# A five-part attention stack on one core: the transfers that are not urgent move from SyncE's queue to GpSimd's, the rows of ones and selectors are filled by DMA instead of by VectorE copies, and VectorE makes the bf16 splits of the first two sets

## What is computed

```python
x = L0(x, ctx)   # 8 heads; LayerNorm of x and of ctx first; x + attention
x = L1(x, ctx)   # 16 heads; causal, keys and queries masked by the valid tokens
x = L2(x, ctx)   # 16 heads; x + attention @ Wo + bo, then x + gelu(x @ W1 + b1) @ W2 + b2
# L3: self attention (causal and padded), then cross attention, then a feed-forward
x = layernorm(mha(x, x) @ Wo1 + bo1 + x)
x = layernorm(mha(x, ctx) @ Wo2 + bo2 + x)
x = layernorm(gelu(x @ W1 + bf1) @ W2 + bf2 + x)
# all in float32; in each attention:
scores = q @ k.T / sqrt(d); probs = softmax(scores + mask); out = probs @ v
```

## Time and profile before

| what | before |
|---|---|
| median of 3 runs | 502.99 us (500.06 to 517.87) |
| the profiled execution | 502.5 us |
| its span, from the first to the last instruction | 500.7 us |
| instructions | 17180 |
| TensorE busy | 447.9 us, 89% |
| VectorE busy | 396.4 us, 79% |
| ScalarE busy | 321.8 us, 64% |
| GpSimd busy | 219.5 us, 44% |
| mean granted clock of TensorE | 0.96 |
| share of the chain that ended last: TensorE, VectorE, DMA, waiting for nothing shown, GpSimd | 72%, 13%, 5%, 4%, 3% |

### The profile page before, as it was taken

The page is one execution under the profiler, slowest core; times in us unless marked ns, Lnnn a source line. Parts: engine busy times, 40 slices in busy tenths (PEclk is TensorE's granted clock), DMA queues, the critical chain, the costliest instruction groups (busy, mean ns, idle before and its releaser), DMA issues.

```text
span 500.7 us, 17180 instructions
## 1 busy us (share of the span) xinstructions
PE 447.9 (89%) x6720; PEld 303.0 (61%) x6720; DVE 396.4 (79%) x1097; ACT 321.8 (64%) x660; POOL 219.5 (44%) x257
## 2 busy tenths in 40 slices
PE   3468869899999988899999999999999999999983
PEld 2356546566666655567777766666666666666762
DVE  7797997868887875879998777878889996777563
ACT  2235746546676654678777776657777787777851
POOL 3475566735722432345444333333443453122245
PEclk9667998999999998999999999999999999999997
DMA  8323434543433444434343232223134432220001
GB/s 189 93 63 98 108 77 92 125 103 99 108 83 79 102 87 89 107 84 96 87 106 74 62 71 65 64 64 76 31 74 93 102 75 65 66 58 14 13 22 31
DMA packets 73138, 39.99 MB, mean 80 GB/s; under 512 B 7168, under 2 KB 72928, under 8 KB 73060
## 3 DMA queue, kind: packets, MB, share of 16 engines
q1 hardware_dynamic: 72952, 38.80, 33.3%
q10 hardware_dynamic: 108, 0.10, 0.1%
HBM read 4.74 MB, written 1.05 MB: 12 GB/s over the span
## 4 chain that ended last, share of the span: by engine, by line
PE 72%; DVE 13%; DMA 5%; issue 4%; POOL 3%; ACT 2%; SPq 1%; POOLq 0%; DVEq 0%; ACTq 0%
PE attn_ps L997 16%; PE o_ps L1024 14%; PE misc_ps L1054 6%; PE misc_ps L1045 5%; PE misc_ps L959 5%; PE misc_ps L1031 4%; DMA pairs<-max_rows 4%; PE score_ps L878 4%; PE misc_ps L960 3%; DVE normed_in L749 3%; DVE max_words L804 3%; PE misc_ps L965 3%; PE misc_ps L1037 2%; PE misc_ps L976 2%; PE misc_ps L1041 2%
## 5 line engine op out<-in xcount | busy, mean ns | idle before, releaser
L804 DVE TENSOR_REDUCE max_words<-score_ps 128x4 f32<-128x512 f32 x288 | 193.7, 683 | 51.9 <-PE score_ps L911 48.9
L693 ACT ACTIVATE probs<-attn_ps 128x512 f32<-128x512 f32 x288 | 169.5, 601 | 79.7 <-PE attn_ps L997 73.8
L997 PE MATMUL attn_ps<-pairs 55*128 55x128 bf16 (+1 forms) x1152 | 114.2, 221 | 9.3 <-DMA pairs<-max_rows 5.6
L911 PE MATMUL score_ps<-pairs 52*128 52x128 bf16 (+1 forms) x1152 | 114.5, 221 | 1.3 <-DVE max_words L804 0.7
L567 POOL TENSOR_TENSOR rest<-qk_f,terms 128x512 f32<-128x512 f32 x40 | 46.9, 1172 | 135.7 <-ACT terms L644 135.7
L997 PEld LDWEIGHTS attn_ps<-pairs 55*128 55x128 bf16 (+1 forms) x1152 | 65.1, 95 | 53.3 <-issue 25.2
L1024 PE MATMUL o_ps<-probs,v 128*32 128x128 f32 x2304 | 97.0, 282 | 0.0
L911 PEld LDWEIGHTS score_ps<-pairs 52*128 52x128 bf16 (+1 forms) x1152 | 66.7, 96 | 4.5 <-DVE max_words L804 1.0
L1024 PEld LDWEIGHTS o_ps<-probs,v 128*32 128x32 f32 x2304 | 53.6, 109 | 23.6 <-issue 9.5
L575 POOL TENSOR_TENSOR terms<-rest,terms 128x512 bf16<-128x512 f32 x40 | 46.3, 1158 | 11.9 <-DVE max_words L817 9.2
L702 ACT ACTIVATE o_sb<-o_ps 128x256 f32<-128x256 f32 x80 | 31.0, 387 | 27.7 <-PE o_ps L1024 26.3
(11 more groups left out here) (108 smaller groups left out, 735.9 us busy)
## 6 DMA issues: line engine op xcount, KB each, us to landing
pairs<-terms SPq DMA_DIRECT2D x240, 128.0 KB
w<-in_weights_dram SPq DMA_DIRECT2D x6, 192.0 KB, 4.1
x_tok<-in_x_dram SPq DMA_DIRECT2D x8, 128.0 KB, 3.4
c_tok<-in_ctx_dram SPq DMA_DIRECT2D x8, 128.0 KB, 5.1
pairs<-max_rows SPq DMA_DIRECT2D x64, 12.0 KB
w<-in_weights_dram SPq DMA_DIRECT2D x8, 128.0 KB, 2.4
out_dram<-x_tok SPq DMA_DIRECT2D x8, 128.0 KB, 1.8
row<-in_rows_dram SPq DMA_DIRECT2D x1, 320.0 KB, 4.1
```

What stands on the lines that cost most here:

```text
L693: act.activation(probs[n % PROBS_RING][:, :, :].rearrange("p h q -> p (h q)"), attn_ps[n % 2][:, :], ACT.Exp, scale=float(D // HEADS[part] ...
L804: dve.tensor_reduce(max_words[ub(step) % 2][:, QUAD * g:QUAD * (g + 1)], score_ps[n % 2][:, :].rearrange("p (h k) -> p h k", h=QUAD), AX_X ...
L911: return pe.matmul(score_ps[NUM[step] % 2][:, j * S:(j + 1) * S], tile[score_rows(u), QUAD * g + j, 0, b * S:(b + 1) * S], tile[score_rows ...
L997: last = pe.matmul(attn_ps[n % 2][:, j * S:(j + 1) * S], pairs[attn_rows(u), h, 1, b * S:(b + 1) * S], pairs[attn_rows(u), h, 0, b * S:(b ...
```

## The change

Six edits. (1) `fill_rows` becomes a transfer: 7 rows (4 for masks, 3 for maxima) of the template, 16 times each, from GpSimd's queue. Two are issued before the first GpSimd step, two behind `ln_in` of set 0. The template is made for one half of the partitions only. (2) The four mask inputs, the second weights, the twelve later pieces of weights and the 20 transfers of mask rows (37 in all) are issued by GpSimd. The mask inputs go behind `ln_in` of set 2, the second weights behind `ln_in` of set 4, the pieces behind `term2` of their unit, the mask rows of units 8 to 11 at the `mask` step of units 0 to 3, and the later ones behind `term2` of their unit, there with a wait for the `attn` of four units before. (3) For units 0 and 1 the three subtractions are VectorE's: the one that gives term 1 stands at `rest`, the one that gives rest at `term1`. (4) Two `v16` tiles are cleared, and the columns of ones set, at `ln_norm` of set 0. (5) The causal masks are made at `ln_in` of set 0. (6) The `mask` steps of units 0 and 2 no longer take part in the shift of 3 and 1 positions that LAG gives these units. SyncE's queue keeps the tokens, the first loads, the stacks, the maxima and the stores.

```diff
@@ schedule
         for kind, pos in PREPARE[part]:
-            put(pos + LAG.get(u, 0), Step(kind, u, 0, 0))
+            put(pos + (0 if kind == "mask" else LAG.get(u, 0)), Step(kind, u, 0, 0))
@@ helpers
-        def fill_rows(dve, r):
-            if r == 0:
-                dve.wait_ge(rows_ready, 5)
-            rows_ = slice(HALF * (r % 2) + QUARTER, HALF * (r % 2 + 1))
-            dve.tensor_copy(pairs16[r // 2][rows_, :, :, :].rearrange("p h a n -> p h (a n)").bitcast(F32),
-                            template[rows_, :, :, :].rearrange("p a b n -> p (a b n)").bitcast(F32).unsqueeze(1)
-                            .to_broadcast([HALF - QUARTER, 16, TOK])).then_inc(fill16_done, 1)
+        def fill_rows(pool, r):
+            first = product_rows(SETS)
+            rows_ = slice(HALF * (r % 2) + first, HALF * (r % 2) + first + MASK_ROWS + TERMS)
+            pool.dma_start(pairs16[r // 2][rows_, :, :, :].rearrange("p h a n -> p h (a n)"),
+                           template[first:first + MASK_ROWS + TERMS, :, :, :].rearrange("p a b n -> p (a b n)")
+                           .unsqueeze(1).to_broadcast([MASK_ROWS + TERMS, 16, 2 * TOK])).then_inc(fill16_landed, 16)
@@ block.sync: the loads, the weights and mask_rows go; stack, c == 0
-                        if u in MASKED_ANEW and u >= SETS + RING:
-                            if part == L1:
-                                sp.wait_ge(mask_l1_ready, u % SETS + 1)
-                            if u == L3S * SETS:
-                                sp.wait_ge(mask_l3_ready, 1)
-                            mask_rows(sp, u)
+                        if u == SETS:
+                            sp.wait_ge(fill16_landed, 16 * RING)
@@ block.gpsimd
+            pool.wait_ge(rows_ready, 3)
+            fill_rows(pool, 0)
+            fill_rows(pool, 1)
             for step in STEPS:
...
+                if step.kind == "mask" and u < RING:
+                    pool.wait_ge(fill16_landed, 16 * RING)
+                    pool.wait_ge(mask_l1_ready, u + 1)
+                    mask_rows(pool, SETS + u)
...
+                if step.kind == "ln_in" and u == 0:
+                    fill_rows(pool, 2)
+                    fill_rows(pool, 3)
+                    pool.memset(causal_t[:, :], 0.0).then_inc(negated_diagonal, 1)
+                    pool.memset(causal_s[:, :], 0.0).then_inc(negated_diagonal, 1)
...
+                if step.kind == "ln_in" and u == 2:
+                    pool.dma_start(validt_raw[:, :], valid_t).then_inc(masks_landed, 16)
...
+                if step.kind == "ln_in" and u == 4:
+                    pool.dma_start(w[:, W_FIRST:W_SECOND, :], weights[:, W_FIRST:W_SECOND, :])\
+                        .then_inc(second_landed, 16)
-                if step.kind == "rest":
+                if step.kind == "rest" and u >= SPLIT_BY_DVE:
                     pool.wait_ge(split1_done, u + 1)
+                    if u == SPLIT_BY_DVE:
+                        pool.wait_ge(split_done, SPLIT_BY_DVE)
...
+                if step.kind == "term2" and part in W_EACH:
...
+                        pool.dma_start(w[:, some, :], weights[:, some, :]).then_inc(weights_landed[user], 16)
+                if step.kind == "term2" and u in MASKED_ANEW and u >= SETS + RING:
+                    freed = the("attn", u - RING, PAIR - 1, HEADS[part] // QUAD - 1)
+                    pool.wait_ge(attn_ready, NUM[freed] + 1)
...
+                    mask_rows(pool, u)
@@ block.vector
                 if kind == "ln_norm" and u == 0:
-                    fill_rows(dve, 0)
-                    fill_rows(dve, 1)
-                if kind == "ln_norm" and u == 1:
-                    fill_rows(dve, 2)
-                if kind == "ln_norm" and u == 2:
-                    fill_rows(dve, 3)
-                if kind == "ln_norm" and u >= SETS - 2:
-                    ring = u % RING
-                    dve.memset(v16[ring][:, :, :], 0.0).then_inc(v_zeroed, 1)
-                if kind == "ln_norm" and u == SETS - 1:
+                    for ring in range(RING // 2, RING):
+                        dve.memset(v16[ring][:, :, :], 0.0).then_inc(v_zeroed, 1)
                     dve.wait_ge(v_zeroed, RING)
...
+                if u < SPLIT_BY_DVE:
+                    terms = terms_ring[u % 2]
+                    if kind == "rest":
+                        dve.wait_ge(split1_done, u + 1)
+                        if u:
+                            dve.wait_ge(split_done, u)
+                        dve.tensor_tensor(terms[:, :, 1, :], qk_f32[:, :, :], terms[:, :, 0, :], ALU.subtract)\
+                            .then_inc(split2_done, 1)
+                    if kind == "term1":
+                        dve.tensor_tensor(rest[:, :, :], qk_f32[:, :, :], terms[:, :, 0, :], ALU.subtract)\
+                            .then_inc(rest_done, 1)
+                    if kind == "term2":
+                        dve.wait_ge(split2_done, u + 1)
+                        dve.wait_ge(rest_done, u + 1)
+                        dve.tensor_tensor(terms[:, :, 2, :], rest[:, :, :], terms[:, :, 1, :], ALU.subtract)\
+                            .then_inc(split_done, 1)
```

78 lines of the change are left out of this document (34 added, 44 removed).

## The result

The changed kernel took 496.61 us (median of 4 runs, 495.54 to 505.73) beside 502.75 for the kernel before (4 runs). The ratio is 0.9873, with a 95% interval of 0.9826 to 0.992: 1.3% faster (6.4 us), within the 2% that count as no change here. 495 was predicted. The profiled execution took 495.54 us against 502.5, its span 493.8 against 500.7. The total came out as forecast; two of the terms behind it did not, and they cancelled.

What follows compares the result with a forecast made beforehand. TensorE was taken to bound 205 to 410 us, VectorE and its waits the start. Terms 4.4 + 2.2 + 1.5 - 0.3 = 7.8 us off the profiled 502.5 gave 494.7, predicted as a 495 us median, range 488 to 505.

Steps and rivals of the forecast that it cites:

- What bounds the kernel: TensorE bounds 205 to 410 us; VectorE and its waits bound the start, whose gain shifts all that follows.
- d: GpSimd's time to issue one transfer, taken as 1.0 us, with 0.7 and 2.3 kept as alternatives.
- Rival C: Start and border to L1: issuing dear on GpSimd, d = 3.0 us, 12.4 us slower, 515 us; chance 0.12.
- VectorE's start: First sets: copies gone, VectorE's statistics and `normed_in` come earlier, set 3's at 28.5 instead of 32.95; 4.4 us gained.
- The clears: Both `v16` clears inside L0 leave the chain of waits: 2 x 1.11, 2.2 us gained.
- SyncE's queue: 37 transfers leave it, maxima are issued earlier and not behind mask rows: 1.5 us gained, bounds 0 and 4.
- GpSimd at the border of L0 and L1: At 87 to 94 us, weights and mask rows make one `rest` 0.7 us late; counted as -0.3 us.
- The sign named for it: Prediction is wrong if GpSimd's idle ahead of `rest` vanishes around L1's first units.
- main case: Whole kernel: the terms sum to 7.8 us gained, 495 us, spanning 490 to 499; chance 0.58.
- A: First two stretches: closing TensorE's gaps raises its clock earlier, 4 us more gained, 491 us; chance 0.15.
- B: Start's gain given back to stacks behind maxima waits or VectorE's score waits; about 3 us stay, 500 us; chance 0.15.
- The two rules: VectorE/GpSimd port lock would give 496.7 us; shared DMA engines, saving only issue time, about 495.8; neither used.

Runs made afterwards that it cites:

- the clears alone: Kernel before with VectorE's `v16` clears moved to the start and nothing else; ratio 0.9972 (0.9937 to 1.0008).
- the mask rows back: Changed kernel with only the mask rows issued by SyncE again; ratio 0.9988 (0.9949 to 1.0027) to the kernel before.
- the place alone: Kernel before with only GpSimd's mask computation placed as in the change, all transfers on SyncE; ratio 0.9991 (0.9954 to 1.0028).
- the transfers without mask rows: Kernel before with weights and mask inputs issued by GpSimd, mask rows on SyncE; ratio 1.0047 (1.0011 to 1.0083).
- the transfers alone: Kernel before with mask rows, mask inputs and weights issued by GpSimd; fills, clears and subtractions as before; ratio 1.0137 (1.0054 to 1.0219).
- late fills: Changed kernel with GpSimd's four fills issued behind the input norms of sets 4 and 5; ratio 0.9846 (0.9786 to 0.9906) to the kernel before.
- transfers and clears alone: Kernel before with mask rows, mask inputs and weights issued by GpSimd and VectorE's clears moved to the start; ratio 0.9977 (0.9936 to 1.0018).

## Why the prediction was right in its sum and wrong in two terms

**What bounds the kernel.** Held. From 205 to 410 us nothing moved (202.50 busy at 1.00, for 202.40 in the earlier trace rows); what was gained came before unit 19, and all but 1.2 us of it was still there at unit 39.

**d.** Taken at 1.0 between 0.7 and 2.3; measured 0.55 to 0.74 for mask rows, mask inputs and weights, and 0.86 at most for a fill (two at 3.85 took 1.51). It is the nearest row (0.707), the lower end, that was right. GpSimd's first `rstd` came at 5.90 us. Rival C, at 3.0, falls with it.

**VectorE's start: 4.4 predicted, 0.9 measured.** All its durations held: clears out by 10.75 (10.8), a subtraction 0.69 (0.70), the pairs of sets 1 and 2 at 0.60, 2.78 us from the first statistic to `normed_in`. The step that failed is "so the statistics of set 1 start at 10.8": they started at 15.26. It took set 1's tokens as landed because they "are issued early", and they share the DMA engines with the fills, which the prediction priced by their issue (2d) and never by their transfer. Set 3's `normed_in` came at 32.03, not at 28.5. With the fills out of the way it came at 26.52 and unit 1 was ahead by 6.6 us; so the estimate of the engines' part was, if anything, low, and what was missing is the price of the transfer.

**The clears: 2.2 predicted.** The lead grows by 2.3 us between units 5 and 7, and by 3.4 when the clears are moved alone. But the same stretch also grows by 1.6 us with only the place of the mask computation moved, and by 2.4 with the mask rows on GpSimd and both clears still in L0, so how much of the 2.3 is the clears' is not shown. In the ratios the clears alone are worth 0.3%, within noise.

**SyncE's queue: 1.5 predicted, bounds 0 and 4; 5.5 to 5.8 measured** by the run that puts the mask rows back, above the upper bound. The place was right and the mechanism too ("issued 0.7 us earlier, and no longer lies behind mask rows"); the term was mis-sized. The prediction had 7.6 us of waits for maxima in its rows and no row for a bound of 4. The waits fell to 2.3 us, and with the mask rows back they are 5.4 and 2.2, 7.6 again. A wait also cost more than its length: at the border the run with the mask rows back waits 1.9 us, and in the window at the same place its TensorE is busy 8.30 us at a clock of 0.83. At 1.00 that work would take 1.4 us less (an estimate from these two numbers); 1.9 and 1.4 make the 3.3 us by which its border gains less than the change's (2.3 for 5.5). The rest of the mask rows' part lies ahead of it: at unit 17 the change is 3.0 us further.

The other 2.2 us of the border's 5.5 are not the mask rows'. The kernel before has two stops there:

```profile
PE attn_ps L878 <- issue: 2.2, 1, 2.2
PE attn_ps L878 <- DMA pairs<-max_rows: 1.8, 1, 1.8
```

These are the waits of 165 to 205 us. The stop of 2.2 us, in which TensorE waits for nothing that the profile shows, is in none of the other traces at this border. Four of these have the mask rows in SyncE's queue too (the clears alone, the place alone, the mask rows back, the transfers without mask rows), and each of the four gains 2.0 to 2.3 us there over the kernel before. So this part belongs to one execution of the kernel before, or to a timing that each of these changes upsets. It ended 5.3 us after a maximum was issued (184.85 to 190.16), as the stop of 1.8 us had ended 5.2 us after its own maximum (173.08 to 178.27), so it may be the same kind of wait; that is not shown.

**GpSimd at the border of L0 and L1: -0.3 predicted, -0.4 measured** (lead 2.7 at unit 8, 2.3 at unit 9). The sign named for it came: the idle time ahead of `rest` is gone at 85.96 and at 93.12 us. What it did was not to make `rest` late but to put it beside VectorE's work. In the timeline after:

```profile
92.42 0.67 POOL L397 DMA_DIRECT2D pairs<-mask_rows_l  x1 [0.67 <-POOL mask_rows_l L498]
...
93.12 1.17 POOL L560 TENSOR_TENSOR rest<-qk_f,terms 128x512 f32<-128x512 f32 x1
93.16 2.27 DVE L833 TENSOR_TENSOR max_words<-max_words 128x8 f32<-128x8 f32 x1
```

GpSimd's issue puts its subtractions beside VectorE's step on the maxima, which takes 2.27 us (1.15 in the kernel before, 0.17 when free). In the change this is the small term predicted; in the run with the transfers alone it went with a loss of 14 us, more than the 9.0 (4.7 and 4.3) that rival C puts there, at issues of 0.7 us instead of its 3.0.

**The rest.** The end of the span gives back 1.4 us that no term had, and units 19 to 39 another 1.2. The sum of the terms is 7.8; the two profiled executions differ by 7.0, of which 2.2 are the stop that only the kernel before shows, and the ratio says 6.4. The start was 3.5 us too high, the queue 4 too low, the losses behind unit 19 were not in the sum. That the forecast was met is luck: its errors cancelled. Nor do the terms simply add: the mask rows are worth 1.15% in the changed kernel, while all the transfers together show no gain in the ratios on top of the clears alone (0.9977 and 0.9972).

**The range and the signs.** The lower end of the main case, "490 (all of the queue's 4 us)", does not follow: 4 instead of 1.5 is 2.5 us below 495, 492.5. One sign of the prediction failed: from set 8's scores to the end the span was to shrink by no more than 2 us; it shrank by 3.9 (the lead is 3.0 at set 8's first scores, 100.08 for 103.05, and 6.9 at the end), which is the queue's term again.

**The rivals.** A: the clock did not come up (0.72 and 0.90 for 0.76 and 0.90). B: in the change the start's gain hardly came, and with late fills it was given back by the fills. The waits that B named were not what did it, but the place was SyncE's queue: with the mask rows back, 6.4 us at unit 1 were lost on set 0's stacks.

**The two rules.** By the exclusive lock of VectorE and GpSimd (the Trainium skill, SBUF — State Buffer, "SBUF: two separate sides") an issue on GpSimd can be held by a VectorE operation. The mask inputs were issued at 24.14 to 26.55 beside `normed_in` of set 2, which took 0.60, and the issues took 0.55 to 0.67, so nothing was held there. Between the engines' own operations the traces agree with the lock: with the transfers alone, VectorE's 3.19 us ended with GpSimd's second subtraction. The shared DMA engines (the Trainium skill, DMA: Bandwidth & Descriptors, "Issuing engines are not separate DMA queues"): for the mask rows the 0.7 us worked out by that rule was too little by far, for the fills it was the thing to read.

**What stays open.** Why a fill weighs so much (the DMA engines are 0.86 busy at 120 GB/s between 35 and 40 us with late fills, and 0.45 at 110 GB/s between 40 and 45 us in the kernel before) is not shown: size and shape of a fill were not varied. Why the transfers alone keep the clock low from 100 to 135 us, when waits of the same kind elsewhere do not, and where the last 1 to 2 us of VectorE's subtractions are gained, is open too.

## What to carry to other kernels

A copy replaced by a DMA is not free once its issue is hidden: count the DMA's landing time against every transfer that is in flight beside it, first of all the loads that the faster path now asks for earlier. A wait can cost more than its length where the engine's clock falls behind it: 1.9 us of waits at one place were worth 3.3. Profile each part alone and with the others before adding its gain to theirs, and compare a loss or a gain at one place over several traces: one stop of 2.2 us was in a single execution only. Before work is added to GpSimd, look at which VectorE operations its long two-input operations will then stand beside.

## What the runs showed of the hardware

- GpSimd issued these DMAs in 0.55 to 0.74 us and the fills in 0.62 to 0.86, no dearer than SyncE (0.43 to 0.95 in the kernel before).
- Four transfers of 112 KB to 7 partitions each landed 5.5 to 10.7 us after their issue in the change. Beside them a load of SyncE's queue took 11.50 us to land and an issue up to 5.03; with late fills a stack took 7.99 and a maximum 6.68. From ScalarE's queue they held SyncE's issues for up to 2.88 us and ScalarE's own for 7.64 in four.
- A VectorE operation that ran beside GpSimd's back-to-back two-input operations lasted until they ended: 3.19 us for 0.60, 2.79 for 0.17.
- The span ends 3.7 us behind the last store's issue instead of 2.3 in the change, in which GpSimd issues weights and mask rows both (3.3 with transfers and clears alone); with either of them back on SyncE it is 2.3. Why is not shown.
